# VectorE's order in a step of a gated cross-attention kernel: the clip ahead of the key remainder

## The chip, the cores and the metric

The kernel runs on one core of a Trainium2 chip. The metric is the device time of one execution in microseconds (us), lower is better. The core's engines are TensorE (PE in the profile; PEld is its weight load), VectorE (DVE), ScalarE (ACT), GpSimd (POOL) and SyncE (SP), which run their own instruction streams in order and meet at semaphores.

## The reference, cut to what matters

A block of a Flamingo model with 32 batches: `x` is 32 x 100 x 256, the context `ctx` is 32 x 1444 x 256, 16 heads of 16.

```python
q = proj(layernorm(x), Wq, bq); k = proj(ctx, Wk, bk); v = proj(ctx, Wv, bv)
scores = clip(einsum('bhsd,bhtd->bhst', q, k) / 4, -50, 50)
scores = clip(where(attend, scores, -10000.0), -50, 50)
probs  = softmax(scores)
delta  = layernorm(rs * (einsum('bhst,bhtd->bhsd', probs, v) @ Wo.T + bo)) * gamma + beta
x = x + tanh(g_xattn) * delta
x = x + tanh(g_ffn) * ffn(layernorm(x))     # two gated 256x704 products and one 704x256, quantized
```

## The kernel before, in words

**Tiles.** Each batch's 1444 context rows are cut into NT = 12 tiles of 121 rows, and these into three chunks u = 0, 1, 2 of four tiles. Scores are kept with the context row on the partition, so that a tile's scores for all 16 heads and 100 queries are 121 x 1600 values. ScalarE takes the exponential of them in two halves (`exps`, L619), and VectorE then clips the exponentials between exp(-50) and a bound of each row, exp(50) or the floor for a masked row (`clip`, L860). So the clip and the mask are one VectorE instruction for a tile. TensorE multiplies four clipped tiles at a time with the values (`pv`, L1347), in the steps 1, 5 and 9; the steps 5 and 9 take tiles of the batch itself, step 1 the last four tiles of the batch before.

**Keys and values.** The context is multiplied in a split form: VectorE makes a rounded high part `c_hi` (`split_head`, L821) and a remainder `c_lo` (`split_rest`, L827). For a chunk TensorE does four context items: two key items (`k_item`, L1368, feature halves o = 0 and 1, into PSUM bank `cb[o]`) and then two value items (`v_item`, L1382, which write the same banks `cb[0]`, `cb[1]`). For a key item ScalarE writes the rounded key `k_hi` (`k_head`, L631), and VectorE then reads the bank once more and writes the remainder `k_lo` (`k_rest`, L851: one 128 x 484 instruction and a short accumulator read, which carries the semaphore `k_lo_done`). Only when `k_rest` of half o is done may the value item o start in that bank: `v_item` waits for `k_lo_done` in its first half. ScalarE copies the values out (`v_out`, L640). SyncE moves `k_hi` and `k_lo` into the stacked form that the scores read.

**Steps.** A batch has 12 steps n = 0 to 11, and each engine has its order of a step written out by hand. TensorE does in a step: half of the scores of tile n, the first half of a context item, side work, `pv` in steps 1, 5 and 9, the other half of the scores, the second half of the context item. The context items run ahead: steps 4 to 11 do items 0 to 7 of the next batch (chunks 0 and 1), steps 0 to 3 do items 8 to 11 of the batch itself (chunk 2). So VectorE's `k_rest` stands in the steps 5 and 6 (chunk 0 of the next batch), 9 and 10 (chunk 1) and 1 and 2 (chunk 2 of this batch), and TensorE's value items that wait for them stand a step later: 6 and 7, 10 and 11, 2 and 3. VectorE's step n clips tile n - 1.

**Side work on VectorE.** In step 1 the attention result of the batch before is read from PSUM as soon as `pv` has ended (`attention_read`, L934 and L937; `sums_inverse`, L943 and L945), in step 2 it is scaled (`attention_out`, L951) and the block's output row group is finished (`result`, L1054). Rows are finished in 25 groups of 128; a batch has 100 rows, so some batches have no such group. Steps 3 to 5 carry the layer norms of the delta and of x (L962 to L1017), step 6 the rounding of the next queries (`q_head` L905, `q_rest` L913), steps 9 to 11 and 0 the hidden layer (L1022 to L1047). The batches are called by their number, 0 to 31.

Of the kernel before, what the change touches and what calls it, by code (L numbers as in the profile page):

```python
# [41 lines left out]
def flamingo_block(nc, x, ctxT, maskT, g_xattn, g_ffn, wqT, bq, wkT, bk, wvT, bv, woT, bo,  # L42
# [37 lines left out]
    NCH = 3  # L80
# [12 lines left out]
    ITEM = 4  # L93
# [15 lines left out]
    with es:  # L109
# [146 lines left out]
        def c_slot(b, u):  # L256
            g = b.plus(u)
            before = 3 * b.pair + (3 * b.par + u) // 2
            return g.par, before


        def e_slot(b, n):
            return (NT * b.par + n) % NE
# [12 lines left out]
        def full_group(b):  # L276

            g = S * (b.row + 1) // P - 1
            if b.row < 0 or g < S * b.row // P:
                return None  # L280
            return whole(g, NG if b.base else 0)
# [473 lines left out]
        def _(dve):  # L755
# [16 lines left out]
            def guard(t, signal, steps, b, step):  # L772

                rows_, w = t.shape[0], math.prod(t.shape[1:])

                def shaped(g):
                    g = g[0:rows_, 0:w]
                    return g.rearrange("p (q d) -> p q d", d=HD) if len(t.shape) == 3 else g

                gt, lt, pos = shaped(g_gt), shaped(g_lt), shaped(g_pos)  # L780

                def wait(name):
                    dve.wait_ge(signal, steps.after_row(b, step + name))

                V.tensor_scalar(gt, t, FMAX, None, ALU.is_gt).then_inc(signal, 1)
                V.tensor_scalar(lt, t, -FMAX, None, ALU.is_lt).then_inc(signal, 1)
                V.tensor_scalar(pos, t, 0.0, None, ALU.max).then_inc(signal, 1)
                wait("pos")
                V.scalar_tensor_tensor(t, t, 0.0, pos, ALU.min, ALU.add).then_inc(signal, 1)
                wait("nan")  # L790
                alone()
                V.copy_predicated(t, gt, shaped(big_pos)).then_inc(signal, 1)
                wait("put_gt")
                alone()
                V.copy_predicated(t, lt, shaped(big_neg)).then_inc(signal, 1)
                wait("put_lt")
# [33 lines left out]
            def watched(b, i, rows_=P):  # L830
                return watch[0:rows_, bass.ds(b.row, 1), i:i + 1].rearrange("p b i -> p (b i)")

            def k_rest(b, u, o):
                slot, n = c_slot(b, u)
                w = CL[u]
                dve.wait_ge(k_hi_done, KE.after(b, f"{u}{o}"))
                if b.base:
                    for i, p in enumerate(pieces):
                        cols = slice(p.start, min(p.stop, w))
                        t = g_k[:, 0:cols.stop - cols.start]  # L840
                        hi, lo = k_hi[slot][:, o, cols], k_lo[slot][:, o, cols]
                        V.tensor_scalar(t, cb[o][:, cols], bk_c[:, o:o + 1], None, ALU.add).then_inc(care_k, 1)
                        dve.wait_ge(care_k, GUARD_K.after_row(b, f"{u}{o}{i}sum"))
                        guard(t, care_k, GUARD_K, b, f"{u}{o}{i}")
                        V.tensor_copy(hi, t).then_inc(care_k, 1)
                        dve.wait_ge(care_k, GUARD_K.after_row(b, f"{u}{o}{i}hi"))
                        V.tensor_tensor(lo, t, hi.bitcast(f32), ALU.subtract).then_inc(care_k, 1)
                        dve.wait_ge(care_k, GUARD_K.after_row(b, f"{u}{o}{i}lo"))
                    dve.sem_inc(k_lo_done, 1)
                    return  # L850
                V.scalar_tensor_tensor(k_lo[slot][:, o, 0:w], cb[o][:, 0:w], bk_c[:, o:o + 1],  # L851
                                       k_hi[slot][:, o, 0:w].bitcast(f32), ALU.add, ALU.subtract,
                                       accum_out=watched(b, KT * u + o)).then_inc(k_lo_done, 1)

            def clip(b, n):
                dve.wait_ge(exp_done, SCORE.after(b, STEPS * (n + 1) - 1))
                if n == 0:
                    dve.wait_ge(pool_mask, b.n + 1)
                e = e_sb[e_slot(b, n)][0:TL[n], :]
                V.tensor_scalar(e, e, E_LO, hi_b[b.par][0:TL[n], n:n + 1], ALU.max, ALU.min).then_inc(clip_done, 1)  # L860
# [104 lines left out]
            def delta_stats(b):  # L965
                d_wait(b, "dl")
                dv(V.bn_stats(dstat[:, :], dl[:, :]))
# [96 lines left out]
            def batch(b, nxt, prev, nxt2=True, own=True):  # L1064
                c, d = b.plus(1), b.plus(-1)
                gd, ge = full_group(d), full_group(b.plus(-2))
                for n in range(NT):

                    if not b.base and b.row == 1 and n == 3:
                        means()  # L1070
                    if nxt and n % 4 == 1:
                        split_head(c, n // 4)
                    if own and n in (ITEM - 3, ITEM - 2):
                        k_rest(b, NCH - 1, n - (ITEM - 3))
                    if nxt and n > ITEM and (n - ITEM - 1) % 4 < 2:
                        k_rest(c, (n - ITEM - 1) // 4, (n - ITEM - 1) % 4)
                    if nxt and n == 6:
                        q_head(c)
                    if prev:
                        if n == 2:  # L1080
                            attention_out(d)
                        if gd and n in (9, 10):
                            hidden_gate(gd, n - 9)
                    if nxt2 and b.row + 3 < NB and n == 11:
                        x_norm(b.plus(3))
                    if ge and n == 2:
                        result(ge)
                    if n:
                        clip(b, n - 1)
                    elif prev:  # L1090
                        clip(d, NT - 1)
                    if nxt and n == 6:
                        q_rest(c)
                    if nxt and n in (2, 5, 9):
                        split_rest(c, n // 4)
                    if b.base:
                        w = n - (ITEM + 1) + (0 if n > ITEM else NT)
                        if w % 4 >= 2 and (nxt if n > ITEM else own):
                            v_guard(c if n > ITEM else b, w // 4, w % 4 - 2)
                    if ge and n == 0:  # L1100
                        for step in (h_scale, h_round, h_quant):
                            step(ge)
                    if not b.base and b.row == 1:
                        if n in (3, 4, 5, 6, 7, 8):
                            for k in range(KT):
                                (w12_scaled, w12_low, w12_high)[(n - 3) % 3]((n - 3) // 3, k)
                        if n in (9, 10, 11):
                            (w3_scaled, w3_low, w3_high)[n - 9]()
                    if b.row == 0 and n == 1:
                        x_stats(b.plus(2))  # L1110
                        x_aggr(b.plus(2))
                    if b.row == 0 and n == 3:
                        x_norm(b.plus(2))
                    if nxt2 and b.row + 3 < NB and n == 9:
                        x_stats(b.plus(3))
                        x_aggr(b.plus(3))
                    if prev:
                        if n == 1:
                            attention_read(d)
                            sums_inverse(d)  # L1120
                    if gd:
                        if n == 3:
                            delta_out(gd)
                            delta_stats(gd)
                            delta_aggr(gd)
                            delta_gamma(gd)
                        if n == 4:
                            first_sum(gd)
                            x1_stats(gd)
                            x1_aggr(gd)  # L1130
                        if n == 5:
                            x1_norm(gd)
                            x2_max(gd)
                            x2_scale(gd)
                            x2_round(gd)
                            x2_quant(gd)
                        if n in (9, 10):
                            hidden_up(gd, n - 9)
                        if n == 11:
                            h_max(gd)  # L1140
# [480 lines left out]
```

## Time and profile before

| | |
|---|---|
| median of 3 runs | 1319.75 us (1317.11 to 1321.18) |
| the profiled execution | 1317.0 us, its span 1315.2 us |
| mean granted TensorE clock | 0.994 of full speed |
| PE busy | 1292.3 us, 98% of the span |
| DVE busy | 1080.8 us, 82% |
| ACT busy | 951.1 us, 72% |
| POOL busy | 361.1 us, 27% |

The engines' busy times overlap. TensorE is busy in nearly the whole span, so the time is read from TensorE: what makes it wait is added to the end, and what shortens another engine's idle time counts only where TensorE waited for it. A batch takes some 39 to 40 us.

### The profile page before, as it was taken

To read this page: it belongs to the slowest core of one execution; us is meant where nothing else is said; L and a number is where in the kernel's file an instruction comes from. 1 tells how busy PE (TensorE), PEld (TensorE's weight loads), DVE (VectorE), ACT (ScalarE), POOL (GpSimd) and SP (SyncE) were. 2 spreads that over 40 slices of the span, in tenths; PEclk is the share of its full clock that TensorE was granted. 3 is DMA by queue.
4 is the path that set the end of the run, shared out by engine and by line. 5 is a ranking of instruction groups with operands and counts; after the bars stand their busy time and mean duration, and the time that the engine had idled before them with its cause. 6 is when DMAs were issued, how large, how long until landed. Compare 5 with 4: busy or idle time off the path is not lost.

```text
span 1315.2 us, 47323 instructions
## 1 busy us (share of the span) xinstructions
PE 1292.3 (98%) x19836; PEld 1184.1 (90%) x19836; DVE 1080.8 (82%) x2167; ACT 951.1 (72%) x1576; POOL 361.1 (27%) x594
## 2 busy tenths in 40 slices
PE   8999999999999999999999999999999999999995
PEld 7999999999999989999899999999999999998985
DVE  5789888789888789886889886889778889778875
ACT  3877777867677767776867777777777767777761
POOL 3222223231233231222331222331133331122320
PEclk9999999999999999999999999999999999999989
DMA  7977667766767776777766768776777766767630
GB/s 206 254 175 169 172 164 192 192 168 166 180 155 195 189 170 164 172 166 197 183 170 166 177 159 207 174 170 164 177 186 179 178 170 163 181 174 181 150 87 12
DMA packets 121421, 225.39 MB, mean 171 GB/s; under 512 B 29675, under 2 KB 89871, under 8 KB 121199
## 3 DMA queue, kind: packets, MB, share of 16 engines
q1 hardware_dynamic: 106968, 200.58, 62.3%
q0 software_dynamic: 12576, 20.42, 6.6%
q8 instruction: 159, 2.61, 0.9%
q10 hardware_dynamic: 1654, 1.27, 0.4%
q14 instruction: 64, 0.52, 0.1%
HBM read 57.27 MB, written 3.28 MB: 46 GB/s over the span
## 4 chain that ended last, share of the span: by engine, by line
PE 79%; DVE 13%; issue 3%; POOL 2%; SPq 1%; DMA 1%; ACT 1%; ACTq 1%; DVEq 0%; POOLq 0%
PE sc L1327 19%; PE pvb L1347 18%; PE cb L1382 17%; PE cb L1368 16%; PE mb L1447 2%; DVE e_sb L860 2%; PE mb L1415 2%; DVE c_lo L827 1%; DVE k_lo L851 1%; DVE zt L945 1%; SPq L342 1%; PE mb L1425 1%; PE mb L1462 1%; DMA k_st<-k_lo 1%; PE cb L1531 1%
## 5 line engine op out<-in xcount | busy, mean ns | idle before, releaser
L619 ACT ACTIVATE e_sb<-sc 121x800 f32<-121x800 f32 (+1 forms) x768 | 645.4, 845 | 167.7 <-PE sc L1327 156.1
L1327 PE MATMUL sc<-q_st,k_st 96*121 96x200 f32 (+1 forms) x3072 | 468.1, 275 | 2.9 <-ACT e_sb L619 1.4
L1327 PEld LDWEIGHTS sc<-q_st,k_st 96*121 96x121 f32 (+1 forms) x3072 | 411.1, 185 | 32.3 <-issue 7.8
L860 DVE TENSOR_SCALAR e_sb<-e_sb,hi_b 121x1600 f32<-121x1600 f32 (+1 forms) x384 | 403.0, 1054 | 18.7 <-ACT e_sb L619 18.7
L1347 PEld LDWEIGHTS pvb<-e_sb,v_sb 121*32 121x32 f32 x12288 | 264.5, 110 | 30.6 <-issue 26.4
L1347 PE MATMUL pvb<-e_sb,v_sb 121*32 121x100 f32 x12288 | 286.2, 250 | 1.2 <-DVE e_sb L860 1.2
L851 DVE SCALAR_TENSOR_TENSOR k_lo<-cb,bk_c,k_hi 128x484 fp32r<-128x484 f32 (+1 forms) x192 | 134.6, 701 | 125.5 <-ACT k_hi L631 124.9
L1382 PE MATMUL cb<-wv_hi,c_hi 128*121 128x256 f32 (+1 forms) x768 | 223.1, 290 | 2.4 <-DVE k_lo L851 1.2
L505 POOL DMA_DIRECT2D q_st<-bd_hi x256 | 152.3, 598 | 259.0 <-DVE bd_lo L913 252.9
L1382 PE MATMUL cb<-wv_hi,c_lo 128*121 128x256 f32 (+1 forms) x768 | 216.0, 281 | 0.0
L1382 PE MATMUL cb<-wv_lo,c_hi 128*121 128x256 f32 (+1 forms) x768 | 215.7, 281 | 0.0
L1368 PE MATMUL cb<-c_hi,wk_hi 128*128 128x484 f32 (+1 forms) x384 | 153.2, 399 | 1.4 <-ACT v_sb L640 1.4
L1382 PEld LDWEIGHTS cb<-wv_hi,c_hi 128*121 128x121 f32 (+1 forms) x768 | 141.5, 184 | 6.5 <-DVE k_lo L851 6.3
L1368 PE MATMUL cb<-c_hi,wk_lo 128*128 128x484 f32 (+1 forms) x384 | 145.9, 380 | 0.0
L1368 PE MATMUL cb<-c_lo,wk_hi 128*128 128x484 f32 (+1 forms) x384 | 145.5, 379 | 0.0
L1382 PEld LDWEIGHTS cb<-wv_hi,c_lo 128*121 128x121 f32 (+1 forms) x768 | 140.8, 183 | 0.1
L1382 PEld LDWEIGHTS cb<-wv_lo,c_hi 128*121 128x121 f32 (+1 forms) x768 | 140.2, 183 | 0.0
L631 ACT ACTIVATE k_hi<-cb,bk_c 128x484 fp32r<-128x484 f32 (+1 forms) x192 | 127.0, 661 | 2.0 <-PE cb L1368 1.9
L484 POOL TENSOR_TENSOR d_r<-d_ve,minus_half 128x1 f32<-128x1 f32 x25 | 32.2, 1288 | 344.4 <-DVE d_ve L975 344.4
L827 DVE TENSOR_TENSOR c_lo<-c_in,c_hi 128x968 fp32r<-128x968 f32 (+1 forms) x96 | 117.1, 1220 | 0.0
L640 ACT ACTIVATE v_sb<-cb 121x512 f32<-121x512 f32 x160 | 96.2, 602 | 10.1 <-PE cb L1382 10.1
L1368 PEld LDWEIGHTS cb<-c_hi,wk_lo 128*128 128x128 f32 x384 | 72.1, 188 | 11.7
(165 smaller groups left out, 1358.6 us busy)
## 6 DMA issues: line engine op xcount, KB each, us to landing
k_st<-k_hi SPq DMA_DIRECT2D x508, 121.0 KB, 2.5
c_in<-in_ctxT SPq DMA_DIRECT2D x64, 484.0 KB, 3.9
k_st<-k_lo SPq DMA_DIRECT2D x254, 121.0 KB, 2.5
k_st<-k_hi SPq DMA_DIRECT2D x252, 119.0 KB, 3.2
c_in<-in_ctxT SPq DMA_DIRECT2D x32, 476.0 KB, 3.9
k_st<-k_lo SPq DMA_DIRECT2D x126, 119.0 KB, 3.0
q_st<-bd_hi POOLq DMA_DIRECT2D x256, 50.0 KB, 3.4
q_st<-bd_lo POOLq DMA_DIRECT2D x128, 50.0 KB, 3.5
```

Source lines behind the costliest of these rows:

```text
L484: nc.gpsimd.tensor_tensor(d_r[:, :], d_ve[:, :], minus_half[:, :], ALU.pow).then_inc(pool_post, 1)
L505: nc.gpsimd.dma_start(q_st[b.par][QR * part:QR * (part + 1), j, :, :].bitcast(f32), src[QR * j:QR * (j + 1), :, :, :].rearrange("p k a s - ...
L619: nc.scalar.activation(e_sb[e_slot(b, n)][0:TL[n], k * SW:(k + 1) * SW].rearrange("p (o c) -> p o c", o=2), sc[q % NSC][0:TL[n], :, 0:2 * PW],
L631: nc.scalar.activation(k_hi[slot][:, o, 0:CL[u]], cb[o][:, 0:CL[u]], ACT.Identity, bias=bk_c[:, o:o + 1]).then_inc(k_hi_done, 1)
L640: nc.scalar.activation(v_sb[0:TL[n], n:n + 2, :, 0:3:2, :].rearrange("p n q a d -> p (n q) a d"), cb[i][0:TL[n], :].rearrange("p (q a d) - ...
L827: V.tensor_tensor(c_lo[slot][:, :, 0:w], c_in[slot][:, :, 0:w], c_hi[slot][:, :, 0:w].bitcast(f32), ALU.subtract).then_inc(split_done, 1)
L851: V.scalar_tensor_tensor(k_lo[slot][:, o, 0:w], cb[o][:, 0:w], bk_c[:, o:o + 1], k_hi[slot][:, o, 0:w].bitcast(f32), ALU.add, ALU.subtract ...
L860: V.tensor_scalar(e, e, E_LO, hi_b[b.par][0:TL[n], n:n + 1], ALU.max, ALU.min).then_inc(clip_done, 1)
L1327: last = T_.matmul(sc[q % NSC][0:TL[n], e // 2, (e % 2) * PW:(e % 2 + 1) * PW], k_st[st_slot(b, n // TPC)][:, pr % NQ, pr // NQ, t0:t0 + T ...
L1347: last = T_.matmul(pvb[QR * j:QR * (j + 1), col:col + S], v_sb[0:TL[n], n, pr, a:a + 2, :].rearrange("p x d -> p (x d)"), e[0:TL[n], pr * ...
L1368: last = T_.matmul(cb[o][:, 0:w], wt[:, k, o * P:(o + 1) * P], ct[slot][:, k, 0:w], start=i == 0, stop=i == 5)
L1382: last = T_.matmul(cb[i][0:TL[n], half * H:(half + 1) * H], ct[slot][:, k, t0:t0 + TL[n]], wt[:, k, :], start=(k == 0 and a == 0), stop=(k ...
```

## The change

In VectorE's `batch` the two lines that call `k_rest` move from ahead of `q_head`, `attention_out`, `hidden_gate`, `x_norm`, `result` and `clip` of the step to behind them. No instruction is added or removed, no wait, no other engine's order changes.

```diff
                         split_head(c, n // 4)
-                    if own and n in (ITEM - 3, ITEM - 2):
-                        k_rest(b, NCH - 1, n - (ITEM - 3))
-                    if nxt and n > ITEM and (n - ITEM - 1) % 4 < 2:
-                        k_rest(c, (n - ITEM - 1) // 4, (n - ITEM - 1) % 4)
                     if nxt and n == 6:
                         q_head(c)
...
                     elif prev:
                         clip(d, NT - 1)
+                    if own and n in (ITEM - 3, ITEM - 2):
+                        k_rest(b, NCH - 1, n - (ITEM - 3))
+                    if nxt and n > ITEM and (n - ITEM - 1) % 4 < 2:
+                        k_rest(c, (n - ITEM - 1) // 4, (n - ITEM - 1) % 4)
                     if nxt and n == 6:
                         q_rest(c)
```

VectorE, step 2 of a batch that finishes a row group (the third batch; L945 is the last instruction of step 1, L951 the scaled attention result, L1054 the output, L860 the clip, L851 the key remainder):

```order
 L945 RECIPROCAL zt<-zt 128x200
-L851 SCALAR_TENSOR_TENSOR k_lo,watch<-cb,bk_c,k_hi 128x476
 L951 TENSOR_TENSOR oT<-pT,zt 128x2x56
 L951 TENSOR_TENSOR oT<-pT,zt 128x2x44
 L1054 SCALAR_TENSOR_TENSOR y_out<-mb,tiny,x 128x256
 L860 TENSOR_SCALAR e_sb<-e_sb,hi_b 121x1600
+L851 SCALAR_TENSOR_TENSOR k_lo,watch<-cb,bk_c,k_hi 128x476
 L827 TENSOR_TENSOR c_lo<-c_in,c_hi 128x968
```

The remainder of half 1 of chunk 2, for which the value item of step 3 waits, moved behind three or four instructions. In a batch that finishes no group L1054 is not there.

VectorE, steps 5 to 6, the end of the norm work and the remainder of half 1 of chunk 0, for which the value item of step 7 waits:

```order
 L1013 TENSOR_SCALAR dn<-dl,tiny 128x256
 L1017 TENSOR_SCALAR x2q<-dn 128x256
+L905 CAST bd_hi<-bd 128x400
+L860 TENSOR_SCALAR e_sb<-e_sb,hi_b 121x1600
 L851 SCALAR_TENSOR_TENSOR k_lo,watch<-cb,bk_c,k_hi 128x484
-L905 CAST bd_hi<-bd 128x400
-L860 TENSOR_SCALAR e_sb<-e_sb,hi_b 121x1600
 L913 SCALAR_TENSOR_TENSOR bd_lo,watch<-bd,bd_hi 128x400
```

It moved behind the query rounding and the clip.

## Rows read from the trace of the kernel before

**Rows 1.** The page: busy time and share of the engines; shares of the last chain.
```profile
PE 1292.3 (98%) x19836; PEld 1184.1 (90%) x19836; DVE 1080.8 (82%) x2167; ACT 951.1 (72%) x1576; POOL 361.1 (27%) x594
...
PE 79%; DVE 13%; issue 3%; POOL 2%; SPq 1%; DMA 1%; ACT 1%; ACTq 1%; DVEq 0%; POOLq 0%
```
**Rows 2.** The waits: who waited <- for whom: us in total, times, longest us.
```profile
DVE k_lo L851 <- ACT k_hi L631: 124.9, 85, 3.9
...
DVE pT L934 <- PE pvb L1347: 24.5, 31, 1.6
...
PEld cb L1382 <- DVE k_lo L851: 6.3, 21, 0.6
```
**Rows 3.** Timeline, VectorE, batch 15, steps 1 to 3: start, us, instruction [idle before].
```profile
621.83 0.43 DVE L934 TENSOR_SCALAR pT<-pvb,submask 128x200 f32<-128x200 f32 x1 [1.56 <-PE pvb L1347]
...
623.43 0.38 DVE L943 STREAM_SHUFFLE zt<-zt 128x200 f32<-128x200 f32 x1
623.85 1.40 DVE L945 RECIPROCAL zt<-zt 128x200 f32<-128x200 f32 x1
625.17 0.62 DVE L851 SCALAR_TENSOR_TENSOR k_lo<-cb,bk_c,k_hi 128x476 fp32r<-128x476 f32 x1
625.71 0.08 DVE L851 DVE_READ_ACCUMULATOR k_lo<-cb,bk_c,k_hi 128x1 f32 x1
625.71 0.36 DVE L951 TENSOR_TENSOR oT<-pT,zt 128x200 f32<-128x200 f32 x1
625.99 1.05 DVE L860 TENSOR_SCALAR e_sb<-e_sb,hi_b 121x1600 f32<-121x1600 f32 x1
626.95 1.16 DVE L827 TENSOR_TENSOR c_lo<-c_in,c_hi 128x968 fp32r<-128x968 f32 x1
...
628.99 0.42 DVE L962 SCALAR_TENSOR_TENSOR dl<-mb,bo_t 128x256 f32<-128x256 f32 x1
```
**Rows 4.** Timeline, TensorE, batch 15, step 3: first value matmul and the delta product.
```profile
625.85 0.38 PE L1382 MATMUL cb<-wv_hi,c_hi 128*121 128x256 f32 x1
...
626.66 1.03 PE L1425 MATMUL mb<-wo,oT 128*128 128x256 f32 x4
```
**Rows 5.** Timeline, batch 16, step 2 of VectorE, and step 3's first value matmul.
```profile
664.25 0.61 DVE L851 SCALAR_TENSOR_TENSOR k_lo<-cb,bk_c,k_hi 128x476 fp32r<-128x476 f32 x1
...
664.79 0.43 DVE L951 TENSOR_TENSOR oT<-pT,zt 128x72 f32<-128x72 f32 x2
...
665.14 0.48 DVE L1054 SCALAR_TENSOR_TENSOR y_out<-mb,tiny,x 128x256 f32<-128x256 f32 x1
...
665.53 1.04 DVE L860 TENSOR_SCALAR e_sb<-e_sb,hi_b 121x1600 f32<-121x1600 f32 x1
...
665.60 0.29 PE L1382 MATMUL cb<-wv_hi,c_hi 128*121 128x256 f32 x1
```
**Rows 6.** Timeline, batch 15, step 6 of VectorE, and step 7's first value matmul.
```profile
638.55 0.72 DVE L851 SCALAR_TENSOR_TENSOR k_lo<-cb,bk_c,k_hi 128x484 fp32r<-128x484 f32 x1
...
639.19 0.36 DVE L905 CAST bd_hi<-bd 128x400 fp32r<-128x400 f32 x1
...
639.33 0.38 PE L1382 MATMUL cb<-wv_hi,c_hi 128*121 128x256 f32 x1 [0.20 <-DVE k_lo L851]
...
639.47 1.04 DVE L860 TENSOR_SCALAR e_sb<-e_sb,hi_b 121x1600 f32<-121x1600 f32 x1
```
**Rows 7.** Timeline, batch 16, step 6 of VectorE, and step 7's first value matmul.
```profile
678.23 0.72 DVE L851 SCALAR_TENSOR_TENSOR k_lo<-cb,bk_c,k_hi 128x484 fp32r<-128x484 f32 x1
...
679.95 0.29 PE L1382 MATMUL cb<-wv_hi,c_hi 128*121 128x256 f32 x1
```
**Rows 8.** Timeline, batch 15, step 10 of VectorE, and step 11's first value matmul.
```profile
651.09 0.72 DVE L851 SCALAR_TENSOR_TENSOR k_lo<-cb,bk_c,k_hi 128x484 fp32r<-128x484 f32 x1 [0.78 <-ACT k_hi L631]
...
652.74 0.29 PE L1382 MATMUL cb<-wv_hi,c_hi 128*121 128x256 f32 x1
```
**Rows 9.** Groups of VectorE's instructions: the output of a row group.
```profile
L1054 DVE SCALAR_TENSOR_TENSOR y_out<-mb,tiny,x 128x256 f32<-128x256 f32 x25 | 11.9, 474 | 2.2 <-PE mb L1462 2.2
```

## The prediction, made before the changed kernel was run

> **What bounds the kernel now.** I read the page first. TensorE is busy 98% of the span and VectorE 82%, and the chain that ended last is 79% TensorE and 13% VectorE [rows 1]. So VectorE's own idle time is worth nothing by itself; what counts is each place where TensorE waits for VectorE, and how near it is to waiting elsewhere. The waits come next. VectorE stood idle 124.9 us, 85 times, until ScalarE had written `k_hi`, because `k_rest` stood first in its step; TensorE's weight load stood 21 times, 6.3 us in all, until VectorE had written `k_lo` [rows 2]. The first number is what the change can fill; the second says that the remainder is already the last thing that TensorE waits for, in places where there is no spare time. The timeline of single batches then tells which places.
>
> **Where the first number is earned.** The 85 waits lie in the steps 9, 10 and 1, and in the steps 5 and 6 of the batches without norm work. In step 10 of batch 15, `k_rest` waited 0.78 us; its instruction ran 0.72 us from 651.09, and TensorE took the bank at 652.74, 0.93 us later than the remainder ended [rows 8]. Placing the clip in such a gap makes the remainder late by about 0.6 us here (gate 0.44, clip 0.96, less 0.78), under that slack, and VectorE is then ahead. TensorE gains nothing from it: the next thing for which VectorE must be early is `attention_read` of step 1, and there VectorE waited for TensorE's `pv` in 31 of 31 batches, 24.5 us in all [rows 2]. Whatever VectorE has saved by then is lost in that wait. This part I cost at 0, and its cover is that wait, 0.8 us a batch in the mean.
>
> **Where the second number grows.** From `attention_read` on, VectorE works without a pause from step 1 to step 6. Batch 15: it starts at 621.83 when `pv` ends, the reciprocal starts at 623.85, `k_rest` (half 1 of chunk 2) at 625.17, and its accumulator read ends at 625.79 [rows 3]. TensorE's value item of step 3 starts at 625.85, 0.06 us behind that end: it waited [rows 4]. In batch 16 the remainder ended at 664.86 (664.25 and 0.61) and the value item started at 665.60 [rows 5]; with the same 0.06 us of signalling the slack is 0.67 us. I find these two cases and no other in the batches 1 to 31: no slack in the 8 that finish no row group in step 2 (1, 2, 6, 11, 15, 20, 24, 29), 0.64 to 0.68 us in the 23 that do. 23 is also the 25 outputs less two at the end [rows 9]: TensorE's down product in step 2 gives those batches their slack.
>
> **Step 2, worked out.** The change puts L951, L1054 where there is one, and the clip ahead. (a) L951 needs the reciprocal's result. That ends at 625.25; an instruction here starts 0.04 us behind the one that it waits for (623.43 and 0.38, then 623.85), so L951 starts at 625.29, 0.12 us later than `k_rest` did [rows 3]. (b) L951 takes 0.28 us up to the next start (0.35 in two pieces), L1054 0.39, the clip 0.96 [rows 3, 5]. (c) `k_rest` behind a clip takes the usual 0.72 us, against 0.62 behind the reciprocal [rows 3, 6]. Without L1054 the remainder ends at 0.12 + 0.28 + 0.96 + 0.72 = 2.08 us where it ended at 0.62: **1.46 us later**, and with no slack TensorE stands 1.46 us longer. With L1054 it ends 1.85 us later, less 0.67: **1.18 us**. Queued behind the waiting value item are TensorE's delta product and the scores of step 3. The delta product of batch 15 ended at 627.69; 1.46 later is 629.15. VectorE reads it at 628.99, and would now come at 629.21, since VectorE's own chain to that point has grown by 0.12 + 0.10 us [rows 3, 4]. They meet, and I add nothing for it. SyncE's stacking of `k_hi` and `k_lo` behind `k_rest` also waits for TensorE's scores of step 3, so it shifts with TensorE.
>
> **Step 6, worked out.** `k_rest` of half 1 of chunk 0 moves behind L905 (639.19 to 639.47, 0.28 us) and the clip (0.96): 1.24 us, and the chain from step 2 brings it 0.22 more, 1.46 in all. In batch 15 TensorE waited here too: 639.33 is 0.06 behind the remainder's end at 639.27 [rows 6]. In batch 16 the end is 678.95 and the value item came at 679.95, slack 0.94 us [rows 7]; even batches have an extra query product in step 5. But these delays do not add to those of step 3. VectorE runs this stretch without waiting for TensorE, so the remainder of step 6 ends at a fixed time behind `attention_read`, and TensorE, already 1.18 or 1.46 us late from step 3, has used most of the time. A batch loses the larger: where step 7 has no slack, 1.46; elsewhere what step 3 cost. No slack at step 7 is found in 11 batches, the odd ones with norm work (3, 7, 9, 11, 13, 15, 17, 21, 25, 27, 29), three of which are among the 8.
>
> **The sum.** 8 batches x 1.46 = 11.7; 8 further odd batches x 1.46 = 11.7; the other 15 x 1.18 = 17.7; two-piece L951 in 12 batches at 0.07 = 0.8; batch 0, a clip against 0.83 us of slack, 0.1. In all 42 us. The steps 6, 10, 11 and 2 (the value items behind the other four remainders) have more slack than their delay of 0.3 to 1.0 us. Against the profiled execution's 1317.0 us that is 1359; against the median of the runs, 2.75 us higher, 1362. I take 1361.
>
> **A rule weighed.** L951 now waits for the instruction right ahead of it. The rows put its start 0.12 us later than that of `k_rest`, which started 0.08 us before the reciprocal's end [rows 3]. The Trainium skill, "VectorE: DVE Perf Modes", section "The DRAIN you can't avoid", has a semaphore after each of a chain of copies cost nothing extra. By that rule the 0.12 us falls away in all 31 batches.
>
> **The rivals.**
> 1. The stalls add up: if TensorE's delay in step 3 holds VectorE back at the delta product or later, the 11 odd batches pay both, 8 x (1.18 + 1.24) + 3 x (1.46 + 1.24) = 27.5 in place of 16.1. For it: the two meet within 0.1 us (629.15 and 629.21). Against it: then it is 0.1 and not 1.2. Time 1361 + 11 = 1372.
> 2. The delays are smaller than the rows say, say 1.0 us a batch, because L951 and L1054 overlap more or TensorE's items have slack that I don't see: 31 us, 1350.
> 3. Waiting costs nothing on VectorE: without the 0.12 us in 31 batches the sum is 38 us, 1357. That is the result of the page's rule named above. Against it: 31 of 31 instructions that follow the shuffle start 0.04 us behind its end and none ahead of it.
> 4. The other side, faster or no change: the 124.9 us of filled idle time carry over into step 1, VectorE reaches `k_rest` of step 2 early enough, and TensorE's 6.3 us of waits go, 1313 us. It decides at `attention_read`: it would need TensorE's `pv` to end before VectorE is free. 31 of 31 waits there speak against it.
> 5. The compiled order is not what the source says. The order of VectorE's rows shows the move at each place, so I give it nothing.
>
> **How the numbers follow.** The forecast (40 to 45 us) 68%, rival 1 10%, rival 2 10%, rival 3 7%, rival 4 5%. 0.3%, some 4 us, is about what a measurement of this kernel can tell from no change. Faster by more 2%, within 3%, slower 95%. The range takes in the forecast, rivals 1 to 3 and the 2.75 us between profile and median, and leaves out rival 4 and the far tails: 1347 to 1374.
>
> **What would show it.** In the profile after: the wait of VectorE for `k_hi` falls from 124.9 us to under 30; TensorE's wait for `k_lo` grows from 6.3 us to about 45, with 40 or so waits; in step 3 of every batch the value matmul starts 0.06 us behind the remainder's end, with 1.2 to 1.5 us of idle time; in step 7 only odd batches wait, 0.3 us or less more than before; `attention_read` still waits for `pv` everywhere; the granted clock stays at full speed, 2.4 GHz. Wrong would be: idle time in step 7 of over 1 us (rival 1), a VectorE pause between step 1 and 6, or TensorE's idle time in steps 2, 6, 10 or 11.

## The result and the profile after

The changed kernel takes 1364.03 us (median of 4 runs, 1362.92 to 1365.09) against 1318.43 us before (4 runs, 1315.49 to 1321.18): a ratio of 1.0344, 95% interval 1.0322 to 1.0366. It is slower by 45.6 us, where the sum had 42: inside the stated range, and just above the 40 to 45 us of the forecast. The profiled execution has a span of 1361.5 us against 1315.2, 46.3 us more, close to the difference of the medians, so the two traces can be laid side by side.

From the page: busy time of the engines, and the granted TensorE clock in tenths over 40 slices. The counterpart before is [rows 1].

```profile
PE 1300.9 (96%) x19836; PEld 1188.7 (87%) x19836; DVE 1089.0 (80%) x2167; ACT 951.1 (70%) x1576; POOL 372.9 (27%) x594
...
PEclk9999999999999999999999999999999999999998
```

The waits (who waited <- for whom: us in total, times, longest), against [rows 2]:

```profile
DVE e_sb L860 <- ACT e_sb L619: 108.4, 149, 2.3
...
PEld cb L1382 <- DVE k_lo L851: 46.6, 43, 1.9
DVE pT L934 <- PE pvb L1347: 45.1, 31, 2.1
DVE th L1022 <- ACT gs L691: 43.1, 49, 2.3
PE cb L1382 <- DVE k_lo L851: 38.8, 42, 1.7
...
DVE k_lo L851 <- ACT k_hi L631: 3.4, 1, 3.4
```

VectorE's 124.9 us of waiting for `k_hi` are gone, and nothing came of it: VectorE now waits longer elsewhere, for the exponentials ahead of the clip (18.7 us before, 108.4 now), for ScalarE in the hidden layer at L1022 (7.3 and 43.1) and for `pv` at `attention_read` (24.5 and 45.1, still in all 31 batches). TensorE's weight load now waits 46.6 us for `k_lo`, against 6.3.

Batch 15, step 2 of VectorE and step 3 of TensorE, from the timeline (start, us, instruction), against [rows 3, 4]:

```profile
645.50 1.40 DVE L945 RECIPROCAL zt<-zt 128x200 f32<-128x200 f32 x1
...
646.81 0.57 PE L1327 MATMUL sc<-q_st,k_st 96*121 96x200 f32 x4
646.94 0.37 DVE L951 TENSOR_TENSOR oT<-pT,zt 128x200 f32<-128x200 f32 x1
647.23 1.05 DVE L860 TENSOR_SCALAR e_sb<-e_sb,hi_b 121x1600 f32<-121x1600 f32 x1
648.19 0.71 DVE L851 SCALAR_TENSOR_TENSOR k_lo<-cb,bk_c,k_hi 128x476 fp32r<-128x476 f32 x1
648.82 0.08 DVE L851 DVE_READ_ACCUMULATOR k_lo<-cb,bk_c,k_hi 128x1 f32 x1
648.82 1.16 DVE L827 TENSOR_TENSOR c_lo<-c_in,c_hi 128x968 fp32r<-128x968 f32 x1
648.96 0.38 PE L1382 MATMUL cb<-wv_hi,c_hi 128*121 128x256 f32 x1 [1.58 <-DVE k_lo L851]
```

The remainder ends 3.40 us after the reciprocal's start (648.90 less 645.50), where it was 1.94 us (625.79 less 623.85): 1.46 us later, and the value item 0.06 us behind it.

The same batch, step 6 of VectorE and step 7 of TensorE, against [rows 6]:

```profile
661.65 0.71 DVE L851 SCALAR_TENSOR_TENSOR k_lo<-cb,bk_c,k_hi 128x484 fp32r<-128x484 f32 x1
...
662.42 0.38 PE L1382 MATMUL cb<-wv_hi,c_hi 128*121 128x256 f32 x1 [0.18 <-DVE k_lo L851]
```

TensorE waits here no longer than before (0.20 us in this batch), though this remainder too is later on VectorE's chain. I laid the start of each batch's value items of the two traces side by side and summed the growth of each stretch:

| stretch of TensorE, over all batches | growth, us |
|---|---|
| from the value item of step 2 to that of step 3 | 39.6 |
| step 3 to step 6 | 4.9 |
| step 6 to step 7 | 0.8 |
| step 7 to the next batch's step 2 | 0.3 |
| start and batch 0's first value item | 0.6 |

The single batches have 1.16 to 1.28 us in the first line where there is an output and 1.45 to 1.54 where there is none. The 4.9 us are two things that the sum had not. In the batches with an output it is 0.06 to 0.11 us: a value item that waited starts up slower, its first matmul taking 0.38 us where one that followed on took 0.29 us. (The batches without an output had waited before the change too, with the 0.38 us of [rows 4], and show no such growth.) And in the batches 6 and 29 it is 1.6 us each, which is the clock. Busy time, granted clock (PEclk, a share of full speed) and DMA in three windows of batch 6, the first of which holds the stall:

```profile
275.00:279.30 4.30, 2.74 (x25) 2.56 (x23) 4.07 (x10) 3.59 (x6) 0.00 (x0) 1.00 0.45 115
279.30:283.30 4.00, 3.91 (x16) 3.55 (x17) 2.74 (x7) 0.00 (x0) 0.00 (x0) 0.57 0.39 114
283.30:287.00 3.70, 3.70 (x28) 3.43 (x27) 3.12 (x9) 3.64 (x8) 1.31 (x1) 1.00 0.48 109
```

TensorE stood 1.65 us, and for most of the next four (mean 0.57) it was granted the lower of its two levels, 1.2 GHz, before it was back at 2.4 GHz.

### The profile page after: what moved, and what is told of

It is laid out like the page before. It is cut to its first block, busy times and chain, and to the rows that moved or that the text cites. A ratio compares the mean times of both kernels' runs of the same rounds, so it can differ in the third digit from the quotient of the medians.

```text
span 1361.5 us, 47323 instructions
## 1 busy us (share of the span) xinstructions
PE 1300.9 (96%) x19836; PEld 1188.7 (87%) x19836; DVE 1089.0 (80%) x2167; ACT 951.1 (70%) x1576; POOL 372.9 (27%) x594
## 3 DMA queue, kind: packets, MB, share of 16 engines
q10 hardware_dynamic: 1654, 1.27, 0.4%
## 4 chain that ended last, share of the span: by engine, by line
PE 71%; DVE 22%; issue 2%; SPq 1%; POOL 1%; ACT 1%; DMA 1%; ACTq 1%; DVEq 0%; POOLq 0%
PE pvb L1347 18%; PE sc L1327 17%; PE cb L1368 15%; PE cb L1382 15%; DVE e_sb L860 4%; DVE zt L945 3%; DVE k_lo L851 3%; PE mb L1447 2%; DVE c_lo L827 2%; PE mb L1415 2%; SPq L342 1%; PE mb L1425 1%; POOL d_r L484 1%; DVE pT L934 1%; DVE zt L943 1%
## 5 line engine op out<-in xcount | busy, mean ns | idle before, releaser
L860 DVE TENSOR_SCALAR e_sb<-e_sb,hi_b 121x1600 f32<-121x1600 f32 (+1 forms) x384 | 404.2, 1053 | 110.9 <-ACT e_sb L619 108.4
L505 POOL DMA_DIRECT2D q_st<-bd_hi x256 | 155.4, 611 | 267.7 <-DVE bd_lo L913 262.8
L1382 PEld LDWEIGHTS cb<-wv_hi,c_hi 128*121 128x121 f32 (+1 forms) x768 | 142.3, 185 | 46.7 <-DVE k_lo L851 46.6
L851 DVE SCALAR_TENSOR_TENSOR k_lo<-cb,bk_c,k_hi 128x484 fp32r<-128x484 f32 (+1 forms) x192 | 136.7, 712 | 3.5 <-ACT k_hi L631 3.4
L827 DVE TENSOR_TENSOR c_lo<-c_in,c_hi 128x968 fp32r<-128x968 f32 (+1 forms) x96 | 111.1, 1157 | 0.0
```

The lines of the kernel that those rows point to most:

```text
L505: nc.gpsimd.dma_start(q_st[b.par][QR * part:QR * (part + 1), j, :, :].bitcast(f32), src[QR * j:QR * (j + 1), :, :, :].rearrange("p k a s - ...
L827: V.tensor_tensor(c_lo[slot][:, :, 0:w], c_in[slot][:, :, 0:w], c_hi[slot][:, :, 0:w].bitcast(f32), ALU.subtract).then_inc(split_done, 1)
L1382: last = T_.matmul(cb[i][0:TL[n], half * H:(half + 1) * H], ct[slot][:, k, t0:t0 + TL[n]], wt[:, k, :], start=(k == 0 and a == 0), stop=(k ...
```

## The experiments

My theory: the time is the delay of one remainder, that of step 2, on VectorE's chain that starts when `pv` ends; the one of step 6 costs little beside it, and the other four nothing. The rivals: the six moves add up, or the filled idle time is worth something somewhere. The engines' line numbers in these kernels are two or a few higher than before for what stands behind the edit.

**The move in step 2 alone.**

```diff
-                    if own and n in (ITEM - 3, ITEM - 2):
-                        k_rest(b, NCH - 1, n - (ITEM - 3))
+                    if own and n == 1:
+                        k_rest(b, NCH - 1, 0)
...
                         clip(d, NT - 1)
+                    if own and n == 2:
+                        k_rest(b, NCH - 1, 1)
```

> Only the remainder of half 1 of chunk 2 (step 2) moves behind the clip; the other five stand where they stood. Theory (the time is the delay of this one remainder, on VectorE's chain that starts when pv ends): 8 batches at 1.45 us and 23 at 1.18 us, some 39 us, with what the clock takes in the changed kernel 40 to 44 us over the kernel before, so nearly all of the 45 us; TensorE does not wait in step 7. Rival (the moves add up over the steps, each some 7 us): under 15 us.

Measured: 1362.8 us against 1319.37, ratio 1.0316 (1.0290 to 1.0342), some 43 us. The waits of its trace:

```profile
DVE k_lo L851 <- ACT k_hi L631: 147.1, 97, 4.4
PEld cb L1384 <- DVE k_lo L851: 43.3, 34, 1.8
```

One of six moved remainders makes nearly all of the cost. VectorE's wait for `k_hi` is not filled here, it is even longer, and the time is nearly that of the changed kernel: that wait has nothing to do with it. In its trace step 3 grew by 39.7 us, as in the changed kernel, while TensorE's small waits of step 7 went, 2.7 us in the 11 odd batches: being late, it no longer reached the remainder of step 6 too early. Three batches (6, 15 and 29) had a stretch at the lower clock.

**The move in step 6 alone.**

```diff
-                    if nxt and n > ITEM and (n - ITEM - 1) % 4 < 2:
+                    if nxt and n != 6 and n > ITEM and (n - ITEM - 1) % 4 < 2:
...
                         clip(d, NT - 1)
+                    if nxt and n == 6:
+                        k_rest(c, 0, 1)
```

> Only the remainder of half 1 of chunk 0 (step 6) moves behind the query rounding and the clip. Theory: alone it costs what it hardly costs beside the move in step 2: 11 odd batches x 1.24 us and 11 even ones x 0.30 us (1.24 less 0.94 of slack), 17 us over the kernel before. With the 39 to 44 us of the move in step 2 the two would be 58, and the changed kernel has 45: the delays don't add. Rival (step 6 is hidden in any case): under 4 us.

Measured: 1337.75 us, ratio 1.0146 (1.0122 to 1.0170), some 18 us. The waits:

```profile
PEld cb L1384 <- DVE k_lo L851: 22.2, 27, 1.7
PE cb L1384 <- DVE k_lo L851: 15.9, 15, 1.5
```

In the trace the stretch up to the value item of step 7 grew by 16.9 us in all: 1.22 to 1.27 us in each of the 11 odd batches, 0.06 to 0.37 in eleven of the even ones with norm work. Those eleven have 2.0 us together where 11 x 0.30 were expected: in most of them VectorE had waited 0.07 to 0.17 us for `k_hi` in step 6 of the kernel before, and the moved instructions fill that wait first. Two batches that the sum had not counted, 1 and 30, bring 0.45 and 0.74 (their slack was 0.80 and 0.49). 43 and 18 are 61, and the two together, with four more moves, cost 45.6. The delays do not add: both remainders lie on one chain of VectorE, and a TensorE that has waited for the first is late enough for the second.

**The other four moves.**

```diff
-                    if own and n in (ITEM - 3, ITEM - 2):
-                        k_rest(b, NCH - 1, n - (ITEM - 3))
-                    if nxt and n > ITEM and (n - ITEM - 1) % 4 < 2:
-                        k_rest(c, (n - ITEM - 1) // 4, (n - ITEM - 1) % 4)
+                    if own and n == 2:
+                        k_rest(b, NCH - 1, 1)
+                    if nxt and n == 6:
+                        k_rest(c, 0, 1)
...
                         clip(d, NT - 1)
+                    if own and n == 1:
+                        k_rest(b, NCH - 1, 0)
+                    if nxt and n in (5, 9, 10):
+                        k_rest(c, (n - ITEM - 1) // 4, (n - ITEM - 1) % 4)
```

> The remainders of the steps 1, 5, 9 and 10 move behind the clip, those of the steps 2 and 6 stay. Theory: no difference, within 2 us of the kernel before, though VectorE's wait for k_hi falls by over 80 us, because attention_read still waits for pv in all 31 batches. Rival (the idle time that is filled is worth something): 4 us or more faster. Rival (late remainders cost here too): 5 us or more slower.

Measured: 1318.9 us against 1319.37, ratio 0.9992 (0.9980 to 1.0005): no difference. The waits:

```profile
DVE e_sb L860 <- ACT e_sb L619: 56.9, 105, 2.5
DVE pT L934 <- PE pvb L1351: 47.1, 31, 2.1
DVE th L1022 <- ACT gs L691: 42.4, 49, 4.6
...
DVE k_lo L851 <- ACT k_hi L631: 30.6, 11, 4.4
```

(This trace is of the slowest of 13 executions, 1325.4 us.) VectorE's wait for `k_hi` fell from 124.9 to 30.6 us, and its other waits took that up: for the exponentials 38 us more, at L1022 35 us more, for `pv` 23 us more. The first two come earlier in the batch; the last is the cover that the prediction named. It holds, since VectorE still waits for `pv` in all 31 batches, but only a quarter of the saved time gets as far as `attention_read`.

**What each part of step 2 weighs.** The remainder behind the scaled result and the output, but ahead of the clip (the line that called it is cut as in the move in step 2 alone; only the new place is shown):

```diff
+                    if own and n == 2:
+                        k_rest(b, NCH - 1, 1)
                     if n:
                         clip(b, n - 1)
```

> Of the move in step 2 only the part past L951 and L1054: the remainder stands behind the scaled attention result and the output, and ahead of the clip. Theory, by the terms of the prediction: a batch without an output 0.12 + 0.28 + 0.72 - 0.62 = 0.50 us, one with an output 0.39 more less 0.67 of slack, 0.22 us: 8 x 0.50 + 23 x 0.22, some 9 us over the kernel before, 10 with the 12 two-piece results; against the 43 us of the move behind the clip as well, the clip is then worth 33 us or 1.06 a batch. No stretch at half the clock. Rival (the whole cost is the clip): under 3 us.

Measured: 1329.08 us against 1319.00, ratio 1.0077 (1.0063 to 1.0092), 10 us. Step 3 grew by 9.7 us in the trace: 0.21 to 0.30 us in the batches with an output, 0.49 to 0.57 in those without. The terms of the sum hold one by one. Against the move behind the clip, 39.7 us in step 3, the clip is worth 30.0 us, which is 31 times the 0.96 us of [rows 3]; the expectation's 33 us, or 1.06 a batch, counted in what the clock took.

**The remainder later still,** behind the clip and `c_lo` (again only the new place is shown):

```diff
                     if nxt and n in (2, 5, 9):
                         split_rest(c, n // 4)
+                    if own and n == 2:
+                        k_rest(b, NCH - 1, 1)
```

> The step 2 remainder stands behind the clip and also behind c_lo of the same step (1.08 us to the next start). Theory: each of the 31 stalls of TensorE in step 3 grows by 1.08 us, 33 us more than with the remainder right behind the clip, so some 74 to 78 us over the kernel before. Second question, the clock: in the changed kernel two of the 8 stalls of 1.75 us were followed by some 4 us at a granted clock of 0.57 and 0.66, which cost 1.6 us each, and none of the 23 of 1.2 us. If the length of the stall decides it, stalls of 2.3 to 2.8 us bring it in most batches and up to 50 us more (1440 us); if it comes by chance, it stays at two or three batches.

Measured: 1426.33 us, ratio 1.0807 (1.0783 to 1.0831), 107 us. Step 3 grew by 73.2 us, 2.24 to 2.62 a batch in the batches 1 to 30, as the chain says (1.18 and 1.46, each with 1.08 more). The stretch from step 3 to step 6 grew by 41.6 us: mostly 1.5 to 1.7 us in each of 24 batches, and some 0.1 us in those where the clock stayed up. Three windows of batch 6, in the order of the ones above: in the stall, behind it, after that:

```profile
249.80:252.30 2.50, 0.43 (x5) 0.26 (x3) 2.50 (x5) 1.40 (x3) 0.00 (x0) 1.00 0.00 0
253.00:256.50 3.50, 3.50 (x19) 3.43 (x18) 1.86 (x3) 1.91 (x4) 0.00 (x0) 0.54 0.82 232
256.70:259.00 2.30, 2.30 (x17) 2.08 (x16) 0.00 (x0) 1.84 (x4) 0.00 (x0) 1.00 0.86 193
```

I counted in six traces which of TensorE's waits for `k_lo` were followed within 4 us by value or key matmuls of the long duration (0.41 us in place of 0.28, 0.5 and more in place of 0.38):

| idle time before the value item | waits | followed by the lower clock |
|---|---|---|
| 0.5 to 1.3 us | 62 | 0 |
| 1.3 to 2.0 us | 22 | 6 |
| 2.0 us and more | 30 | 24 |

The traces are the changed kernel's and those of the five kernels so far. The longer the stall, the more often the lower clock followed; six of the 30 longest stalls passed without it, so the length is not all. One such stretch costs 1.4 to 1.7 us here. The 30 stalls of the last row are all of this one kernel, in step 3; it differs from the kernel with the move in step 2 alone, where 3 of 31 stalls brought the lower clock, only by where that remainder stands and so by the length of these stalls. One of the six in the middle row is a stall of 1.51 us in step 7 of the kernel with the move in step 6 alone, so it is not bound to step 3.

**The other way round.** If the remainder is what TensorE waits for, placing it earlier must help. In the batches without an output the step 2 remainder goes before the reciprocal of step 1, in the odd batches with norm work the step 6 remainder goes into step 5 (the conditions at the old places, not shown, leave these out):

```diff
+                if between:
+                    between()
                 av(V.reciprocal(zs[:, :, :], zs[:, :, :]))
...
+                            if own and not ge:
+                                sums_inverse(d, lambda: k_rest(b, NCH - 1, 1))
+                            else:
+                                sums_inverse(d)
...
                             x2_max(gd)
+                            if nxt and b.row % 2:
+                                k_rest(c, 0, 1)
                             x2_scale(gd)
```

> The other way round: in the batches without an output the step 2 remainder stands before the reciprocal of step 1, and in odd batches with norm work the step 6 remainder stands in step 5 behind the maximum of x2 (its k_hi is there by then). Theory: TensorE's waits of 0.2 to 0.4 us in step 3 (8 batches) and in step 7 (11 batches) go, 3 to 6 us faster than the kernel before, 0.2 to 0.45%. Rival (the work moved behind, the rounding of x2 or the scaled result, becomes what TensorE waits for): no difference or slower.

Measured: 1316.05 us against 1319.00, ratio 0.9980 (0.9967 to 0.9993): 3 us faster, the lower end of what was expected. In the trace 2.1 us were won in step 3 and 2.7 in step 7, and 2.7 lost between step 3 and step 6. I took the clip of tile 3, for which TensorE's `pv` of step 5 waits, for the cause of that loss, and made two more kernels.

> Of the kernel with the two remainders placed earlier only the second part: in odd batches with norm work the remainder of step 6 stands in step 5 behind the maximum of x2, the step 2 remainder stays. The trace of the kernel with both showed 2.1 us won in step 3 and 2.7 us lost again in step 5, where the clip of tile 3 comes 0.3 us late for pv. Theory: so this part alone gives what both gave, 3 us (0.2%) faster than the kernel before. Rival (the step 2 part carries the gain): no difference.

The edit is the last part of the diff above alone. Measured: 1314.59 us against 1318.90, ratio 0.9968 (0.9955 to 0.9982), 4 us faster, no less than with both, so the step 7 part carries the gain. In its trace step 7 won the same 2.7 us, and nothing was lost between step 3 and step 6.

The other one has both parts, and this edit on top of them:

```diff
                             delta_aggr(gd)
-                            delta_gamma(gd)
                         if n == 4:
+                            delta_gamma(gd)
                             first_sum(gd)
```

> Both remainders earlier, and L978 (dn) moves behind the clip of tile 3, so that this clip starts 0.39 us earlier; the next norm instruction waits for GpSimd in that time anyway. Theory: TensorE's 0.34 us of wait before pv in step 5 goes too in the 8 batches without an output, and the 2.1 us of step 3 are kept: 5 to 6 us (0.4%) faster than the kernel before. Rival (the chain of the norm work grows by the moved instruction and comes late for step 7): no more than 3 us.

Measured: 1314.91 us against 1318.90, ratio 0.9978 (0.9965 to 0.9990), no better than the kernel with both parts and without this edit (0.9980), so my cause was wrong. TensorE's waits for the clip became fewer (3 in place of 8), yet the loss between step 3 and 6 stayed at 2.7 us. The eight waits that I had taken for the loss stood in the kernel before as well; its row, and that of the kernel with both parts:

```profile
PEld pvb L1347 <- DVE e_sb L860: 3.8, 8, 1.4
...
PEld pvb L1354 <- DVE e_sb L860: 3.8, 8, 1.4
```

The timeline of the last kernel, batch 15, step 4 (L1375 is the key item, L1414 the transpose of x, L964 the first norm instruction):

```profile
631.00 0.41 DVE L964 SCALAR_TENSOR_TENSOR dl<-mb,bo_t 128x256 f32<-128x256 f32 x1
631.34 0.08 DVE L964 DVE_READ_ACCUMULATOR dl<-mb,bo_t 128x1 f32 x1
...
631.10 0.38 PE L1375 MATMUL cb<-c_hi,wk_lo 128*128 128x484 f32 x1
631.57 0.36 PE L1414 MATMUL mb<-identf,xn 100*128 100x100 f32 x2
```

From the start of the one matmul to that of the other it is 0.47 us, where 0.22 are usual. The transpose writes bank `mb` and by the code waits until VectorE has read the delta product out of it, which ends at 631.42. Laid side by side with the kernel before the change, matmul by matmul, this trace shows the same in seven of the eight batches without an output: the transpose falls back by 0.25 us, 1.8 us in all, and the delta product, which waits for L951, by 0.1 to 0.2 us ahead of that. In the eighth, batch 1, the key item of step 4 falls back by 0.33 us, where the waits name `c_lo`, another instruction of VectorE. The kernel with both parts and without the edit shows the same jumps. So in those batches VectorE's chain, not the one remainder, is the bound: up to L964 it is 0.2 us longer with the remainder before the reciprocal (7.35 us from the start of `attention_read` in place of 7.16 in batch 15), since L951 now stands right behind the reciprocal for whose result it waits, and all that step 3 won is lost again by step 6.

## Why the prediction was right

**Which number of the waits counts.** Right in the part that decides the time. 124.9 us of idle time filled gave nothing (the four moves alone: ratio 0.9992), and the 6.3 us were the sign of the loss.

**The delays of step 2.** Right to 0.02 us: 1.46 and 1.18 us were worked out, and the trace of after has 1.45 to 1.54 and 1.16 to 1.28, the upper ones where L951 is in two pieces. The term of 0.12 us for L951 as well: it started 0.04 us behind the reciprocal's end (646.90 and 646.94). By the rule of the Trainium skill's page "VectorE: DVE Perf Modes", section "The DRAIN you can't avoid", the semaphore would have cost nothing; here the trace does not agree, by that 0.12 us against an instruction that does not wait. (The page speaks of copies, and no run here has a chain of them.)

**Step 6 and no adding up.** Right in kind: alone 18 us, beside step 2 some 2 to 3 (45.6 against 43.4 by the medians). Rival 1 fell with it, rivals 2 and 3 fell with the delays of step 2, rival 4 with the sign of the result; the delta product met VectorE's read without a wait, as worked out for batch 15. The size was not quite right: the sum gave 0.28 us more to 8 odd batches, 2.2 us, and the stretch to step 7 grew there by 0.09 to 0.21 us each, 1.3 us, because part of the delay had already come with the slower start after the stall. Over all batches it was 0.8, since batch 29, late from the clock, lost its wait.

**The clock.** Wrong, a term that the sum lacked. I had written that it would stay at full speed and had no term for it. The traces show two stretches of some 4 us behind stalls of 1.65 us, 3.2 us in all. With 1.9 us of slower starts, which the sum had not either, this is 5.1 us, and with the 1.4 us too many for step 7 it gives the difference between 42 and 46: two misses of opposite sign, so a part of the closeness of 42 is luck. In both batches VectorE then waited for the late delta product (1.22 us in batch 6, 0.49 in batch 29), the pause between step 1 and step 6 that the prediction had named as a sign of being wrong. The row of before that I had for it was a mean clock of 0.994 in a kernel in which TensorE's idle gaps from 66 to 1262 us were all under 0.5 us; it said nothing about stalls three times as long.

**Where the idle time went.** Partly foreseen. I expected it at `attention_read`, which took 21 us more; most of it, 90 us, went to the clip, which now stands where `k_rest` stood and waits for the exponentials, and 36 us to L1022. It changes nothing in the time.

**Even batches in step 7.** They do not wait, as said, but the slack fell from 0.94 to 0.53 us. By the prediction's terms 0.28 us of it were to go. In nine of these batches the clip of step 6 now waits 0.34 to 0.38 us for the exponentials, which makes the remainder behind it later: here VectorE does pause. Its unpaused run from step 1 to step 6, read from batch 15, did not hold for every batch before the change either: those without norm work stood 0.7 us for `k_hi` in step 5. In the 11 odd batches, for which the sum uses it, it holds in the kernel after too, but for batch 29 and its clock.

**The idle time in step 3.** TensorE stood 1.0 to 1.7 us in front of the value item, where 1.2 to 1.5 had been named; the growth of the stretch, which is what counts, was as worked out.

## What to carry to other kernels

An idle time that an engine off the bound spends waiting is worth only what the bound engine gets from it; look for the shortest slack between a producer and the bound engine before moving a producer back, and count every instruction that it is moved behind. Delays at several places of one chain were not summed here: the bound engine paid the largest once, because the delayed engine did not wait for it between these places. Where the bound is TensorE, look at the length of single stalls too: the longer ones here were often charged again by the clock. And before a wait is called the cause of a loss, see whether it stood in the trace before as well.

## What the runs showed of the hardware that I had not expected

In six traces, of TensorE's stalls before a value item, none of 0.5 to 1.3 us was followed by the lower clock (62 cases), and 24 of the 30 of 2 us and more were. The stretches shown lasted some 3 to 4 us, and most cost 1.5 to 1.7 us. With the remainder behind `c_lo` this was a third of the loss: of 107 us some 73 are the stalls and most of the rest the clock. And a value item that had waited starts slower than one that follows on, 0.38 us for its first matmul against 0.29, some 0.09 us a stall.
